# Cross-attention over pairs of batches: where the probabilities are transposed, and how the squares of the norms are summed

## What is computed

```python
text_p = jnp.einsum('bld,dh->blh', H_l, W_text) + b_text
audio_p = jnp.einsum('bsd,dh->bsh', H_a, W_audio) + b_audio
Q = layer_norm(text_p, g1, beta1)
K = layer_norm(audio_p, g2, beta2)
scores = jnp.einsum('blh,bsh->bls', Q, K) * scale
alpha = jax.nn.softmax(scores, axis=-1)
H_hyper = jnp.einsum('bls,bsh->blh', alpha, audio_p)
H_hyper = jnp.einsum('blh,hk->blk', H_hyper, W_out) + b_out
return layer_norm(H_hyper + H_l, g_out, beta_out)
```

## Time and profile before

| | |
|---|---|
| median of 3 runs | 1298.52 us (1298.16 to 1299.54) |
| the profiled execution | 1299.89 us, span 1298.1 us |
| granted TensorE clock, mean | 0.992 |
| busy: TensorE, VectorE, ScalarE, GpSimd | 1270.3, 1164.0, 1001.5, 724.4 us |

### The profile page before, as it was taken

One profiled execution on the slowest core, in us unless ns is written; L12 is line 12 of the kernel. 1 busy time (PEld: TensorE's weight loads), 2 busy tenths in 40 slices (PEclk: granted clock), 3 DMA queues, 4 the chain that ended last, 5 costly groups with the idle time before them and its releaser, 6 DMA issues.

```text
span 1298.1 us, 22641 instructions
## 1 busy us (share of the span) xinstructions
PE 1270.3 (98%) x6704; PEld 1077.7 (83%) x6704; DVE 1164.0 (90%) x2049; ACT 1001.5 (77%) x1655; POOL 724.4 (56%) x757
## 2 busy tenths in 40 slices
PE   7999999999999999999999999999999999999994
PEld 5688888888888888888888888888888888888874
DVE  5689999999999999998999999999998999899987
ACT  6677787887787887787887787887787887787862
POOL 1123666555666555666555666555666555665564
PEclk9999999999999999999999999999999999999997
DMA  7454755566755566755566755666755566755662
GB/s 251 130 119 126 203 174 144 157 188 186 202 183 122 171 187 186 202 173 143 157 189 186 202 179 124 170 189 186 202 174 142 157 190 186 202 182 118 176 175 79
DMA packets 76693, 221.02 MB, mean 170 GB/s; under 512 B 9856, under 2 KB 9856, under 8 KB 68480
## 3 DMA queue, kind: packets, MB, share of 16 engines
q1 hardware_dynamic: 55312, 154.70, 33.7%
q0 software_dynamic: 21360, 66.06, 26.7%
HBM read 121.12 MB, written 33.55 MB: 119 GB/s over the span
## 4 chain that ended last, share of the span: by engine, by line
PE 94%; DVE 3%; ACT 1%; DMA 1%; issue 1%; SPq 1%; DVEq 0%; ACTq 0%
PE wide L294 9%; PE wide L296 9%; PE wide L295 9%; PE scores_both L261 7%; PE scores_both L262 7%; PE scores_both L263 7%; PE wide L341 7%; PE wide L343 7%; PE wide L342 7%; PE wide L263 7%; PE wide L261 7%; PE wide L262 6%; PE turn L305 1%; PE turn L262 1%; PE turn L261 1%; PE turn L263 1%
## 5 line engine op out<-in xcount | busy, mean ns | idle before, releaser
L963 POOL TENSOR_TENSOR y_rows<-y_rows,go_row 128x512 f32<-128x512 f32 x120 | 156.4, 1304 | 216.3 <-ACT y_rows L505 216.3
L658 DVE STREAM_TRANSPOSE scores_both<-probs 32x256 f32<-32x256 f32 x512 | 233.4, 456 | 8.2 <-ACT probs L514 0.2
L294 PE MATMUL wide<-xT_hi,wt_hi 128*128 128x512 f32 x512 | 202.1, 395 | 0.8 <-ACT k_cols L474 0.8
L296 PE MATMUL wide<-xT_hi,wt_lo 128*128 128x512 f32 x512 | 202.1, 395 | 0.0
L295 PE MATMUL wide<-xT_lo,wt_hi 128*128 128x512 f32 x512 | 201.8, 394 | 0.0
L943 POOL DMA_DIRECT2D xT_lo<-xT_in x31 | 27.9, 899 | 248.1 <-ACT xT_lo L447 248.1
L965 POOL TENSOR_TENSOR y_rows<-y_rows,betao_row 128x512 f32<-128x512 f32 x120 | 155.7, 1297 | 9.4
L473 ACT ACTIVATE squares<-wide,bac_col 128x512 f32<-128x512 f32 x128 | 88.2, 689 | 90.3 <-PE wide L263 90.3
L341 PE MATMUL wide<-wao_hi,pcT_hi 128*128 128x512 f32 x384 | 153.4, 400 | 0.0
L261 PE MATMUL wide<-cT_hi,wa_hi 128*128 128x512 f32 x384 | 152.3, 397 | 0.3 <-DVE wa_lo L782 0.3
L263 PE MATMUL wide<-cT_hi,wa_lo 128*128 128x512 f32 x384 | 152.2, 396 | 0.0
(11 more groups left out here) (120 smaller groups left out, 3570.4 us busy)
## 6 DMA issues: line engine op xcount, KB each, us to landing
xT_in<-in_xT SPq DMA_DIRECT2D x32, 1024.0 KB, 9.6
y_rows<-in_x_rows SPq DMA_DIRECT2D x124, 256.0 KB, 4.4
xT_lo<-xT_in POOLq DMA_DIRECT2D x31, 1024.0 KB, 7.0
y_rows<-bao_row POOLq DMA_DIRECT2D x31, 1024.0 KB, 10.4
out<-y_rows SPq DMA_DIRECT2D x124, 256.0 KB, 2.3
cT_in<-in_cT SPq DMA_DIRECT2D x32, 768.0 KB, 7.7
c_kept<-in_c_rows SPq DMA_DIRECT2D x32, 768.0 KB, 6.8
q_cols<-in_L_xattn_W_text SPq DMA_DIRECT2D x1, 1024.0 KB, 5.8
```

Of the source, the lines that this page charges most:

```text
L294: nc.tensor.matmul(wide[h][:], wt_hi[:, d, cols], xT_hi[:, d, :], start=(d == 0), stop=False)
L296: done = nc.tensor.matmul(wide[h][:], wt_lo[:, d, cols], xT_hi[:, d, :], start=False, stop=(d == DT - 1))
L658: done = nc.vector.transpose(to[Q * b:Q * (b + 1), :, Q * a:Q * (a + 1)], of[Q * a:Q * (a + 1), :, Q * b:Q * (b + 1)])
L963: nc.gpsimd.tensor_tensor(rows, rows, go_row[:], ALU.mult).then_inc(y_scaled, 1)
```

## The change

It has five parts. (1) VectorE transposes all of probs, which is now laid out with the 32-column groups outermost, by one instruction in place (`turn_p`): every 32 x 32 square is turned where it lies. Then SyncE's queue moves the squares between the partition quarters by 16 DMAs of 32 x 256 elements into pT_lo (`exchange_p`); `pT_high` and `pT_low` read them from there, once for both batches. (2) The sum of squares is halved: ScalarE copies its upper 64 partitions into PSUM (`move_half`), VectorE adds them to the lower 64 (`halve_sum`), `split_sum` puts the high part on partitions 0 to 63 and the low part on 64 to 127 of sq_parts, and one matmul with mean_of takes both. The places of these matmuls move, too. (3) The output norm: VectorE subtracts the mean and multiplies by g_out (`y_gain`), ScalarE multiplies by the scale alone, GpSimd only adds beta_out. (4) The second batch's exponentials stand at the end of their own step. (5) In the tail, TensorE transposes the last pair's probabilities (`turn_last_p`), and ScalarE and VectorE split them from PSUM (`last_pT_high`, `last_pT_low`).

```diff
-        sq_hi, sq_lo = sb("sq_hi", [P, T * P], F32R), sb("sq_lo", [P, T * P], F32R)
+        sq_parts, sq_half = sb("sq_parts", [P, T * P], F32R), sb("sq_half", [P // 2, T * P])
-        probs = sb("probs", [P, T, S])
-        pT_hi, pT_lo = sb("pT_hi", [P, NB, ST * L], F32R), sb("pT_lo", [P, NB, ST * L], F32R)
+        probs = sb("probs", [P, NQ, T * ST, Q])
+        pT_hi, pT_lo = sb("pT_hi", [P, NQ, T * ST, Q], F32R), sb("pT_lo", [P, NQ, T * ST, Q], F32R)
...
+            def exchange_p(j):
+
+                wait_apart(sp, pc_done, CT * j)
+                wait_apart(sp, p_turned, j + 1)
+                to, of = pT_lo[:].bitcast(F32).rearrange("p a k c -> p a (k c)"), probs[:].rearrange("p b k c -> p b (k c)")
+                for a in range(NQ):
+                    for b in range(NQ):
+                        sp.dma_start(to[Q * b:Q * (b + 1), a, :], of[Q * a:Q * (a + 1), b, :]).then_inc(pT_loaded, 16)
...
-                    for t in range(T):
+                    for t in (0, 1):
+                        store_y(i - 2, odd, t)
+                if not last:
+                    exchange_p(i)
+                if not isinstance(i, int) or i >= 2:
+                    for t in (2, 3):
                         store_y(i - 2, odd, t)
...
-            def mean_squares(i, to, sq_hi_made, sq_lo_made, var):
-
-                pe.wait_ge(sq_hi_made, i + 1)
-                nc.tensor.matmul(to, mean_of[:], sq_hi[:], start=True, stop=False)
-                pe.wait_ge(sq_lo_made, i + 1)
-                nc.tensor.matmul(to, mean_of[:], sq_lo[:], start=False, stop=True).then_inc(var, 1)
+            def mean_squares(i, to, parts_made, var):
+
+                pe.wait_ge(parts_made, i + 1)
+                nc.tensor.matmul(to, mean_of[:], sq_parts[:], start=True, stop=True).then_inc(var, 1)
+
+            def turn_last_p(b):
+
+                pe.wait_ge(probs_made, T * (N - 1) + LT * (b + 1))
+                flat = probs[:].rearrange("p b k c -> p (b k c)")
+                transposes(score[b], [flat[:, ((LT * b + l) * ST + s) * P:((LT * b + l) * ST + s + 1) * P]
+                                      for s in range(ST) for l in range(LT)]).then_inc(last_pT_done, 1)
...
             def turned(of, b, s):
-                return of[:, b, :].rearrange("p (l s c) -> p s l c", l=LT, s=ST)[:, s]
-
-            def probs_context(j, d, batches=range(NB)):
+                return of[:].rearrange("p a (b l s) c -> p b s l a c", b=NB, l=LT)[:, b, s]
+
+            def turned_last(of, b, s):
+                return of[:].rearrange("p a k c -> p (a k c)")[:, (b * ST + s) * L:(b * ST + s + 1) * L]
...
                     project_k(i, h)
                 project_q(i, 0)
-                project_q(i, 1)
-                mean_squares(i, turn[0][:], k_sq_hi, k_sq_lo, k_var)
+                project_q(i, 1, 0)
+                mean_squares(i, turn[0][:], k_sq_parts, k_var)
+                project_q(i, 1, 2)
                 project_q(i, 2)
...
-                mean_squares(i, turn[1][:], q_sq_hi, q_sq_lo, q_var)
+                tiles = range(T - 1 if last else T)
                 if not first:
-
                     pe.wait_ge(q_centred, HT * i + 2)
                     output_part(j, 0, 0)
-                    output_part(j, 0, 1)
                     output_part(j, 1, 0)
+                mean_squares(i, turn[1][:], q_sq_parts, q_var)
                 if not first:
-                    output_part(j, 0, 2)
-                    output_part(j, 1, 1)
-                    output_part(j, 1, 2)
-                    for t in range(2, T - 1 if last else T):
+                    for t in tiles[2:]:
                         pe.wait_ge(q_centred, HT * i + t + 1)
-                        output(j, t)
+                        output_part(j, t, 0)
+                    for t in tiles:
+                        output_part(j, t, 1)
+                        output_part(j, t, 2)
...
+            turn_last_p(0)
             pe.wait_ge(q_centred, HT * N)
             output(N - 2, T - 1)
+            turn_last_p(1)
...
-            def pT_high(j, b):
-                act.wait_ge(pT_done, j + 1)
+            def pT_high(j):
+                wait_apart(act, pT_loaded, 16 * NQ * NQ * (j + 1))
                 wait(act, pc_done, CT * j)
-                nc.scalar.copy(pT_hi[:, b, :], score[b][:]).then_inc(pT_hi_made, 1)
+                nc.scalar.copy(pT_hi[:], pT_lo[:].bitcast(F32)).then_inc(pT_hi_made, 1)
+
+            def last_pT_high(b):
+                act.wait_ge(last_pT_done, b + 1)
+                nc.scalar.copy(pT_hi[:].rearrange("p a k c -> p (a k c)")[:, 512 * b:512 * (b + 1)],
+                               score[b][:]).then_inc(last_pT_hi_made, 1)
...
+
+            def move_half(i, to, summed, moved):
+
+                act.wait_ge(summed, i + 1)
+                nc.scalar.copy(to[P // 2:P, :], squares[P // 2:P, 3, :]).then_inc(moved, 1)
...
             def y_norm(j, odd, t):
-                act.wait_ge(y_scales, T * j + t + 1)
-                nc.scalar.activation(y_rows[odd][:, t, :], y_rows[odd][:, t, :], ACT.Identity,
-                                     scale=y_sc[:, t, 0:1], bias=y_sc[:, t, 1:2]).then_inc(y_normed, 1)
+                if t % 2 == 0:
+                    wait_apart(act, y_rstd, T * j + t + 2)
+                act.wait_ge(y_gained, T * j + t + 1)
+                nc.scalar.mul(y_rows[odd][:, t, :], y_rows[odd][:, t, :], y_sc[:, t, 0:1]).then_inc(y_normed, 1)
...
-                wait(act, pT_done, i)
+                if b == 0:
+                    wait_apart(act, pT_loaded, 16 * NQ * NQ * i)
-                    nc.scalar.activation(probs[:, at, :], score[b][:, l * S:(l + 1) * S], ACT.Exp,
+                    to = probs[:, :, ST * at:ST * (at + 1), :].rearrange("p b s c -> p s b c")
+                    of = score[b][:, l * S:(l + 1) * S].rearrange("p (s b c) -> p s b c", s=ST, b=NQ)
...
                 k_centre(i, 0)
-                if not first:
-                    exponentials(j, 1)
                 k_centre(i, 1)
                 k_centre(i, 2)
                 k_centre(i, 3)
+                move_half(i, turn[0], k_summed, k_moved)
+                rstd_of(i, turn[0], k_var, k_log, k_rstd)
                 if late:
                     y_norm(i - 2, odd, 0)
                 q_centre(i, 0)
-                rstd_of(i, turn[0], k_var, k_log, k_rstd)
                 q_centre(i, 1)
                 if not first:
-                    pT_high(j, 0)
+                    pT_high(j)
                 k_high(i, 0)
                 k_high(i, 1)
-                if not first:
-                    pT_high(j, 1)
                 q_centre(i, 2)
                 k_high(i, 2)
                 q_centre(i, 3)
+                if not first:
+                    pc_high(j, 0)
+                move_half(i, turn[1], q_summed, q_moved)
                 k_high(i, 3)
                 if first:
                     wao_high(0)
                     wao_high(1)
                 else:
-                    for d in range(CT):
-                        pc_high(j, d)
+                    pc_high(j, 1)
+                    pc_high(j, 2)
                 rstd_of(i, turn[1], q_var, q_log, q_rstd)
                 if late:
                     y_norm(i - 2, odd, 1)
@@ -602,6 +647,7 @@
                     y_norm(i - 2, odd, 2)
                     y_norm(i - 2, odd, 3)
                 exponentials(i, 0)
+                exponentials(i, 1)
...
-            def turn_p(j, quadrants):
+            def turn_p(j):
                 dve.wait_ge(probs_made, T * (j + 1))
-                Q = 32
-                of = probs[:].rearrange("p t s -> p (t s)").rearrange("p (k c) -> p k c", c=P)
-                to = scores_both[:].rearrange("p (k c) -> p k c", c=P)
-                for a in quadrants:
-                    for b in range(P // Q):
-                        done = nc.vector.transpose(to[Q * b:Q * (b + 1), :, Q * a:Q * (a + 1)],
-                                                   of[Q * a:Q * (a + 1), :, Q * b:Q * (b + 1)])
-                if a == P // Q - 1:
-                    done.then_inc(pT_done, 1)
-
-            def pT_low(j, b):
-                dve.wait_ge(pT_hi_made, NB * j + b + 1)
-                low(pT_lo[:, b, :], score[b][:], pT_hi[:, b, :]).then_inc(pT_split, 1)
+                flat = probs[:].rearrange("p b k c -> p (b k c)")
+                nc.vector.transpose(flat, flat).then_inc(p_turned, 1)
+
+            def pT_low(j):
+                dve.wait_ge(pT_hi_made, j + 1)
+                low(pT_lo[:], pT_lo[:].bitcast(F32), pT_hi[:]).then_inc(pT_split, 1)
+
+            def last_pT_low(b):
+                dve.wait_ge(last_pT_hi_made, b + 1)
+                half = slice(512 * b, 512 * (b + 1))
+                low(pT_lo[:].rearrange("p a k c -> p (a k c)")[:, half], score[b][:],
+                    pT_hi[:].rearrange("p a k c -> p (a k c)")[:, half]).then_inc(last_pT_split, 1)
...
+            def halve_sum(i, of, moved, halved):
+
```

(25 more changed lines are left out.)

80 lines of the change are left out of this document (49 added, 31 removed).

## The result

The changed kernel takes **1313.88 us** (median, 1312.47 to 1321.85, four runs), the kernel before 1298.83 beside it (1298.16 to 1299.54): a ratio of **1.0125**, 95% interval 1.0105 to 1.0145. Slower by 15 us, where 1290 was forecast. The profiled execution took 1313.13 us around a span of 1311.3, at a mean granted clock of 0.994.

The account below looks back on a forecast made before the run. TensorE, busy 39.00 of 39.00 us per step, was taken as the bound. From the profiled 1299.9: minus 14.9 for matmuls, plus 14.9 for waits, minus 8.5 in the tail, 1291.4; less 1.4, 1290 us. Range 1275 to 1305.

Parts of the forecast that it names:

- Step 5: SyncE's queue: 16 more DMAs per step at 0.44 us, 7 us in all, covered by 4 and 3 us; cost 0.
- Rival C: SyncE's queue: exchange DMAs of 0.75 us each bring the probabilities 1 us late to ScalarE; +31 us, 1321; chance 0.04.
- Steps 1 to 3: Norms, per step: 0.47 us saved in matmuls, waits of 0.28 at k's mean, 0.2 at q's and scores; net 0.0.
- Step 1: Norms on TensorE: two mean matmuls fewer per step at 0.233 us each, 14.9 us saved over 32 steps.
- Step 4: VectorE and GpSimd: one transpose of 1.3 us replaces 16, y_gain and halvings added; about 2 us gained per step, hidden.
- Step 6: The last pair: TensorE transposes replace VectorE's 16, ending most of an 8.91 us wait; 8.5 us saved, between 6 and 10.
- Rival B: k's sums: a GpSimd instruction locks the shared port, holding y_gain and halving by 0.9 us; +28 us, 1318; chance 0.2.

Follow-up runs that it names:

- e6: The changed kernel, its 16 exchange DMAs kept, with x loaded by one DMA on GpSimd's queue and two stores between the exchange's 4th and 5th DMA: 1300.62 us.
- e7: e6 with the halving undone, so two mean matmuls per norm: 1292.09 us.
- e13: e6 with q's first block ahead of k's Ln, k's first high part ahead of the turned probabilities, k's mean behind 19 projection matmuls: 1280.33 us.
- e1: The changed kernel with the exchange made of 4 DMAs of 128 KB instead of 16 of 32 KB, squares landing in wrong places: 1298.12 us.
- e4: e1 with the halving undone: high and low part of the whole sum, two mean matmuls per norm: 1291.17 us.
- e10: e6 with one row scaling and q's first block ahead of k's Ln, k's mean three matmuls later, q's three earlier: 1304.86 us.
- e11: e6 with one row scaling and q's first block ahead of k's Ln, mean matmuls left in place: 1318.95 us.
- e12: The changed kernel with the x loads behind c, cT and xT on SyncE's queue instead of ahead of them: 1352.63 us.

## Why the prediction was wrong

- **Step 5, the queue, is the step that failed,** and it carries the sign. It priced an exchange DMA by the x loads, 0.44, "7 us in all", found cover of 4 and 3 us, and wrote "Cost 0". Measured: 0.63 each, 10.14 us. In the step shown xT was asked for 8.7 us behind k's mean (512.87 against 504.15), where the forecast had 3.6 (500 against 496.4): 3.1 of the difference is the price of the exchange, 1.4 what the stores and loads took between it and xT, 0.5 its later start. The landing took 1.1 us more, too. So the cover of 3 us was gone in ten steps, and TensorE, which the forecast had waiting for none of this, stopped in the scores. bias_x waited for x 29 times, but that cost TensorE little here. Undone by fewer DMAs the step is worth 15.8 us, by moving the loads 13.3.
- **Rival C** had the queue and a price of 0.75 per DMA, but named the probabilities as the victim and gave it 0.04. In the change the probabilities came in time (they are late in e6, e7 and e13). It looked at what the new DMAs deliver, not at what stands behind them. Its sign and its 0.75 came near for a victim that was another one, which is luck.
- **Steps 1 to 3, the norms,** had the mechanism right and a size too small. By e1: 0.25 at k's mean (0.3 forecast), 0.11 at q's (0.1) and 0.30 in the scores (0.2), but the sum rounded the last two to 0.2 together. 0.66 stand against 0.47 saved, where 0.0 net was forecast. What was missing is that a matmul that is waited for costs about 0.1 behind it as well as ahead of it, and step 0, 2.6 us once with the clock. In e1 against e4 that is the 7 us that the halving nets; even without step 5's failure the change would have come to 1298 and not to 1290.
- **Step 1's saving** is real: with the waits out of the way (e13) the step falls by 0.47, as said.
- **Step 4, the hidden work:** the transpose takes 1.23 (1.3 forecast), y_gain 0.75 between sum and halving. A step's first y_gain is held to between 1.31 and 1.91 in 29 of 30 steps, where nothing waits for it (the group's mean is 959 ns). Column chunks of 32 as moving operand cost nothing: the 256-column matmuls keep their pace of 0.12.
- **Step 6, the tail:** 8.1 us alone (8.5 forecast), the granted clock of the change at 1.00 until past its last matmul. Right.
- **Rival B** did not come in the change itself. Its mechanism came in e10 and e11, by an order that looked free, and in e12, through a late load. In e11, 1.1 us of lock per step at k's sum cost 18.3 us net; B asked 28 for 0.9.
